# Two-layer gated decoder, one core: layer 1's down projection as three rounded products, with the weights' low parts streamed

## What is computed

```python
x = x + tanh(g_xattn[0]) * L0_xattn(layernorm(x), ctx, ctx)
# L0_ffn: of each sequence the k = 256 tokens with the highest score
scores = einsum('bld,d->bl', x, w_r) + b_r
_, idx = top_k(scores, k)
x_sel = take_along_axis(x, idx)
h = gelu(einsum('bkd,df->bkf', x_sel, w1) + b1)      # 512 -> 2048
out_sel = einsum('bkf,fd->bkd', h, w2) + b2          # 2048 -> 512: the down projection
out = zeros_like(x).at[batch, idx].set(out_sel)
x = x + tanh(g_ffn[0]) * L0_ffn(layernorm(x))
# then layer 2
```

## Time and profile before

| | us |
|---|---|
| median of 3 runs | 1008.98 |
| lowest, highest | 1005.02, 1009.32 |
| the profiled execution: its time | 1008.89 |
| the profiled execution: its span | 1007.1 |

### The profile page before, as it was taken

The page is one execution under the profiler, slowest core; times in us unless marked ns, Lnnn a source line. Parts: engine busy times, 40 slices in busy tenths (PEclk is TensorE's granted clock), DMA queues, the critical chain, the costliest instruction groups (busy, mean ns, idle before and its releaser), DMA issues.

```text
span 1007.1 us, 15849 instructions
## 1 busy us (share of the span) xinstructions
PE 899.4 (89%) x5592; PEld 586.9 (58%) x5592; DVE 678.4 (67%) x1893; ACT 574.5 (57%) x1098; POOL 82.2 (8%) x101
## 2 busy tenths in 40 slices
PE   3989998999999888799898999899999898999777
PEld 2868775667677463567444566544566544566433
DVE  4996771524241063699786799787699787699793
ACT  4545333455553032689546689547688547688543
POOL 2000213021120003200100000010000010000000
PEclk9999999999999989899999999999999999999979
DMA  6344566443350048710179210169210159300001
GB/s 192 130 159 139 196 230 230 147 141 111 106 206 24 21 152 179 151 43 1 43 153 182 84 43 2 44 131 194 94 43 2 43 117 202 100 1 2 1 1 42
DMA packets 52270, 102.82 MB, mean 102 GB/s; under 512 B 8924, under 2 KB 8924, under 8 KB 50656
## 3 DMA queue, kind: packets, MB, share of 16 engines
q1 hardware_dynamic: 39872, 71.88, 27.3%
q10 hardware_dynamic: 8160, 17.31, 5.2%
q0 software_dynamic: 4160, 12.62, 4.0%
HBM read 55.62 MB, written 14.75 MB: 70 GB/s over the span
## 4 chain that ended last, share of the span: by engine, by line
PE 36%; DVE 9%; issue 6%; ACT 5%; SPq 4%; DMA 3%; POOL 1%; DVEq 0%; ACTq 0%; POOLq 0%
PE psum L1517 7%; PE psum L1485 6%; PE psum L1590 6%; PE psum L1534 5%; PE psum L1560 5%; SPq L1186 4%; ACT probs L1333 3%; DMA k<-k_lo 3%; PE psum L1452 1%; PE psum L1576 1%; PE psum L1543 1%; DVE xn L1911 1%; DVE stats L1906 1%; DVE stats L57 1%; POOL q L1170 1%
## 5 line engine op out<-in xcount | busy, mean ns | idle before, releaser
L1333 ACT ACTIVATE probs<-psum,neg_max 128x512 f32<-128x512 f32 x256 | 174.7, 691 | 46.1 <-DVE neg_max L1801 46.1
L1801 DVE CUSTOM_DVE_ANT_0 psum<-psum,m_in 128x512 f32<-128x512 f32 x256 | 174.0, 704 | 17.2 <-issue 17.2
L1517 PE MATMUL psum<-ident,probs 128*128 128x128 f32 x1024 | 153.3, 274 | 0.0
L1485 PE MATMUL psum<-k,q 128*128 128x512 f32 x256 | 125.1, 494 | 15.5 <-ACT probs L1333 7.5
L1517 PEld LDWEIGHTS psum<-ident,probs 128*128 128x128 f32 x1024 | 127.1, 140 | 19.5 <-issue 1.8
L674 PE MATMUL psum<-w_sb,hT 128*128 128x512 f32 x256 | 117.5, 604 | 5.5 <-ACT hT L566 5.5
L1831 DVE COPY probsT<-psum 128x512 f32<-128x512 f32 x128 | 87.9, 687 | 4.0 <-PE psum L1517 2.8
L1324 ACT COPY probsT<-psum 128x512 f32<-128x512 f32 x128 | 75.1, 587 | 20.4 <-PE psum L1517 20.4
L594 PE MATMUL psum<-xselT_hi,w_hi 128*128 128x256 f32 x256 | 81.8, 320 | 1.6 <-ACT xselT_hi L501 1.6
L1485 PEld LDWEIGHTS psum<-k,q 128*128 128x128 f32 x256 | 48.8, 191 | 52.3 <-ACT probs L1333 32.8
L674 PEld LDWEIGHTS psum<-w_sb,hT 128*128 128x128 f32 x256 | 46.9, 192 | 55.3 <-issue 48.2
(11 more groups left out here) (237 smaller groups left out, 1536.8 us busy)
## 6 DMA issues: line engine op xcount, KB each, us to landing
bw_raw<-in_L_ffn_W_dram ACTq DMA_DIRECT2D x16, 1024.0 KB, 5.3
c_in<-in_ctx_dram SPq DMA_DIRECT2D x8, 1024.0 KB, 5.3
k<-k_hi SPq DMA_DIRECT2D x24, 256.0 KB, 5.9
k<-k_lo SPq DMA_DIRECT2D x24, 256.0 KB, 6.9
q<-q_hi SPq DMA_DIRECT2D x48, 128.0 KB, 3.9
q<-q_lo SPq DMA_DIRECT2D x48, 128.0 KB, 3.5
xres<-in_x_dram SPq DMA_DIRECT2D x4, 1024.0 KB, 5.9
w_raw<-in_L_ffn_w_dram POOLq DMA_DIRECT2D x4, 1024.0 KB, 5.6
```

The source lines that it names most:

```text
L1333: act.activation(probs[:, u % 4, :], psum[u % SCORE_BANKS][:, :], ACT.Exp, scale=-1.0, bias=neg_max[:, u:u + 1], accum_out=prob_sum[:, nt, ...
L1485: pe.matmul(psum[u % SCORE_BANKS][:, :], q4[:, h, nt * P:(nt + 1) * P], k4[:, h, :], start=True, stop=True).then_inc(score_psum, 1)
L1517: mm = pe.transpose(turn_bank(u)[:, l * P:(l + 1) * P], probs[:, u % 4, l * P:(l + 1) * P], ident[:, :])
L1801: dve.tensor_tensor_reduce(bank[:, :], bank[:, :], m_in[:, nt, :], -1.0, LOWEST, ALU.add, ALU.min, neg_max[:, u:u + 1]).then_inc(masked_re ...
```

## The change

1. **Down projection.** `down` becomes `three` on 128x512 tiles: 12 float32r matmuls for a pair where there were 4 float32 ones. ACT makes `h_hi` (`hidden_high`, a 128x512 copy behind each pair's gelu), DVE `h_lo` (`hidden_low`); both lie in a ring of 3.
2. **Weights of it.** `w2_hi` stays in SBUF (ACT, `w2_high`, 8 copies of 128x1024, 3 of them before the first up). The low parts don't fit: for each of the 32 pairs SP loads 512 KB of w2 again (`load_w2`, a ring of 3, each waiting for the down that used the slot, three pairs earlier), and DVE subtracts (`w2_low`, 128x1024).
3. **PE's order.** up(g) for g = 0 to 31 without a break between batches, and down(g - 2) behind it. DVE's additions to `x_sel` (`put_together`) stand behind `hidden_low` of the next batch's pair 1.
4. **DVE's list** is dealt out by pairs (`route_next`, `round_next`): hidden_low, put_together, a piece of the routing, w2_low.
5. **Order of batches** 0, 3, 1, 2 (`ORDER`), since only `xres[0]` stays free of the rings; batches 1 and 2 are loaded again (`load_x1`).
6. **First routing** spread a pair later: PE's `spread_scores` at pair 3, ACT's at pair 4; in later batches pair 2 and 3.
7. **load_selected** moves from SP to POOL.
8. **Hand-over.** The last two scatters move from POOL's list in layer 1 to the head of POOL's list in layer 2. wk is loaded once down(30) has ended (`w2_used`), wv once the last down has; layer 1 no longer waits for either, PE waits before their transposes.

```diff
+                def load_w2(g):
+                    k, p = divmod(g, PAIRS)
+                    if g >= RING:
+                        k0, p0 = divmod(g - RING, PAIRS)
+                        if p0 == PAIRS - 1:
+                            sp.wait_ge(osel_psum, (k0 + 1) * JT)
+                        else:
+                            sp.wait_ge(w2_used, k0 * (PAIRS - 1) + p0 + 1)
+                    i = g % RING
+                    sp.dma_start(w2_raw[:, 2 * i:2 * i + 2, :], w2[2 * P * p:2 * P * (p + 1), :].rearrange("(f p) c -> p f c", p=P)
+                                 ).then_inc(w2_loaded[i], 16)
...
+                sp.wait_ge(w2_used, (B - 1) * (PAIRS - 1) + PAIRS - 2)
+                load_weight(2, wk, sh.wk_loaded)
+                sp.wait_ge(osel_psum, B * JT)
+                load_weight(1, wv, sh.wv_loaded)
...
+                for g in range(RING):
+                    w2_high(g)
                 selected_highs(0)
...
+                for g in range(B * PAIRS):
+                    k, p = divmod(g, PAIRS)
+                    if k + 1 < B and p == (3 if k else 4):
+                        spread_scores(k + 1, psum[4])
+                    gelu(g)
+                    hidden_high(g)
+                    if RING <= g < PAIRS:
+                        w2_high(g)
+                    if k + 1 < B and p == PAIRS - 1:
+                        selected_highs(k + 1)
+                    weights(g)
...
+                def up(g):
+                    k, p = divmod(g, PAIRS)
...
+                    if g >= 2:
+                        pe.wait_ge(h_ready, 2 * (g - 1))
...
+                def down(g):
+                    k, p = divmod(g, PAIRS)
+                    pe.wait_ge(h_lo_ready, g + 1)
+                    pe.wait_ge(w2_lo_ready, g + 1)
+                    if p == 0 and k:
+                        pe.wait_ge(x2_ready, k * JT)
+                    for i in range(2):
+                        f = 2 * p + i
                         for j in range(JT):
-                            mm = pe.matmul(psum[j][:, :], hT[:, f % RING, j * P:(j + 1) * P], w2_sb[:, f, :],
-                                           start=(f == 0), stop=(f == FT - 1))
+                            mm = three(psum[j][:, :], [h[g % RING][:, i, j * P:(j + 1) * P] for h in (h_hi, h_lo)],
+                                       [w2_hi[:, f, :], w2_lo[:, 2 * (g % RING) + i, :]], f == 0, f == FT - 1)
...
+                for g in range(B * PAIRS):
+                    k, p = divmod(g, PAIRS)
+                    up(g)
+                    if k + 1 < B and p == PAIRS - 1:
+                        if k == 1:
+                            pe.wait_ge(bw_inv_ready, 2)
+                        turn_selected(k + 1)
+                    weights(g)
+                    if g >= 2:
+                        down(g - 2)
+                    if k + 1 < B and p == (2 if k else 3):
+                        spread_scores(k + 1, psum[4])
+                down(B * PAIRS - 2)
+                down(B * PAIRS - 1)
...
+                for g in range(B * PAIRS):
+                    k, p = divmod(g, PAIRS)
+                    hidden_low(g)
+                    if k and p == 1:
+                        put_together(k - 1)
+                    if g == 1:
+                        w2_low(2)
+                    if k + 1 < B:
+                        route_next(k, p, link)
...
+                    if g >= RING:
+                        w2_low(g)
+                put_together(B - 1)
...
+                for j in range(sh.ids.shape[2]):
+                    pool.indirect_dma_start(
+                        sh.x_mid[sh.last_batch][:, :], bass.IndirectOffsetOnAxis(ap=sh.ids[:, B - 1, j:j + 1], axis=0),
+                        sh.x_sel_last[:, j, :], None).then_inc(sh.x2_stored[sh.last_batch], 16)
...
-                for i, (w, ready) in enumerate(((wk_in, linear_act_ready), (wv_in, linear_dve_ready))):
+                for i, (w, loaded, ready) in enumerate(((wk_in, sh.wk_loaded, linear_act_ready),
+                                                        (wv_in, sh.wv_loaded, linear_dve_ready))):
+                    pe.wait_ge(loaded, 16)
```

More of the change, by code:

```diff
@@ L168, in layer0 @@
         XW = C + 8
+        RING = 3
+        ORDER = [0] + [B - 1] + list(range(1, B - 1))
         xres = sb("xres", [P, 3, T, C])
@@ L225, in layer0 @@
         xn_sel = at("xn_sel", [P, JT, XW], F32, parts_at + 8 * K)
-        RING = 8
-        hT = at("hT", [P, RING, KEEP], F32, sig_at)
+        h_at = (sig_at, sig_at + 4 * K, sh.front + 20 * K)
+        h_hi = [at(f"h_hi{i}", [P, 2, KEEP], F32R, h_at[i]) for i in range(RING)]
+        h_raw = [at(f"h_raw{i}", [P, 2, KEEP], F32, h_at[i] + 2 * K) for i in range(RING)]
+        h_lo = [at(f"h_lo{i}", [P, 2, KEEP], F32R, h_at[i] + 2 * K) for i in range(RING)]
         score = sb("score", [P, T])
@@ L254, in layer0 @@
         w1_lo_ready = sem("w1_lo_ready")
-        w2_loaded = [sem(f"w2_loaded_{i}") for i in range(4)]
+        w2_loaded = [sem(f"w2_loaded_{i}") for i in range(RING)]
+        w2_hi_ready = sem("w2_hi_ready")
+        w2_lo_ready = sem("w2_lo_ready")
+        w2_used = sem("w2_used")
+        h_hi_ready = sem("h_hi_ready")
+        h_lo_ready = sem("h_lo_ready")
+        x1_loaded = sem("x1_loaded")
         x_loaded = sem("x_loaded")
@@ L379, in _ @@
                 select(0)
+                load_selected(0)
                 fetch(0)
@@ L664, in up @@
                     mm.then_inc(h_psum, 1)
-                def down(b, pair):
-                    pe.wait_ge(h_ready, b * FT + 2 * pair + 2)
-                    if pair == 0 and b:
-                        pe.wait_ge(x2_ready, b * JT)
-                    if b == 0 and pair % 2 == 0:
-                        pe.wait_ge(w2_loaded[pair // 2], 16)
-                    for f in (2 * pair, 2 * pair + 1):
+                def down(g):
[5 more added lines that the diff above has]
+                    for i in range(2):
+                        f = 2 * p + i
@@ L837, in cross_attend @@
                         w1_lows(range(4))
+                        for g in range(2):
+                            w2_low(g)
                     if b == 1:
@@ new lines, in round_weights, with whole_weights @@
+                def round_weights(i, link):
+                    w = (wq_w, wo_w)[i]
+                    for t in range(CT_):
+                        dve.tensor_scalar(w[:, t, :], w[:, t, :], sh.w_inv[:, i, t:t + 1], ROUND,
+                                          ALU.mult, ALU.add).then_inc(link.sem, 1)
+                        link.count += 1
+                def whole_weights(i, link):
+                    link.wait()
+                    if i == 0:
+                        dve.wait_ge(x_sel_ready, B)
+                        dve.wait_ge(x2_stored[ORDER[B - 2]], 16 * JT)
+                    link(dve.tensor_scalar(w_whole[:, i, :, :], (wq_w, wo_w)[i][:, :, :], -ROUND, None, ALU.add))
@@ new lines, in w2_low, with hidden_low @@
+                def w2_low(g):
+                    i = g % RING
+                    dve.wait_ge(w2_loaded[i], 16 * (g // RING) + 16)
+                    dve.wait_ge(w2_hi_ready, min(g + 1, PAIRS))
+                    f = 2 * (g % PAIRS)
+                    dve.tensor_tensor(w2_lo[:, 2 * i:2 * i + 2, :], w2_raw[:, 2 * i:2 * i + 2, :],
+                                      w2_hi[:, f:f + 2, :].bitcast(F32), ALU.subtract).then_inc(w2_lo_ready, 1)
+                def hidden_low(g):
+                    dve.wait_ge(h_hi_ready, g + 1)
+                    dve.tensor_tensor(h_lo[g % RING][:, :, :], h_raw[g % RING][:, :, :],
+                                      h_hi[g % RING][:, :, :].bitcast(F32), ALU.subtract).then_inc(h_lo_ready, 1)
@@ L879, in bw_unit, with put_together @@
                     dve.reciprocal(bw_inv[:, i:i + 1], sh.bw_mean[:, i:i + 1]).then_inc(bw_inv_ready, 1)
[L881 to L889 removed]
+                def put_together(k):
+                    dve.wait_ge(x_sel_ready, k + 1)
+                    for j in range(JT):
+                        dve.wait_ge(osel_psum, k * JT + j + 1)
+                        dve.scalar_tensor_tensor(x_sel[k % 2][:, j, :], psum[j][:, :], gate_f0, x_sel[k % 2][:, j, :],
+                                                 ALU.mult, ALU.add).then_inc(x2_ready, 1)
@@ new lines, in route_next @@
+                def route_next(k, p, link):
+                    n = k + 1
+                    if p == 0:
+                        if n == 1:
+                            route_stats(link, n)
+                        route_norm(link, n)
+                    elif p == 1:
+                        scores(link, n)
+                        if k == 1:
+                            bw_unit(0)
+                    elif p == 2 and k == 0:
+                        w1_lows(range(6, PAIRS))
+                    elif p == 3:
+                        ranks(link, n, range(2))
+                    elif p == 4:
+                        ranks(link, n, range(2, T))
```

253 lines of the change are left out of this document (119 added, 134 removed).

## The result

The changed kernel takes 998.73 us (median of 5 runs, 997.36 to 999.49) where the kernel before takes 1006.09 beside it (5 runs, 1004.70 to 1009.32): a ratio of 0.9915, 95% interval 0.9895 to 0.9935. Set again beside the kernel before in a later comparison it took 997.84 for 1008.16, a ratio of 0.9904 (0.9873 to 0.9934). The forecast was 998, a fall of 11.1; measured is a fall of 7.4 in the first comparison and of 10.3 in the second. The total was right; most of its terms were not, and that they cancelled is luck.

A forecast was written before the change was run, and what follows sets the result against it. It took ACT's chunk chain to set the pace up to M (192.7 us) and PE only behind it. Stage -5.8 and hand-over -5.3 made -11.1 on 1008.89: about 998 us, range 991 to 1004, with the rivals 984 to 1009.

The forecast's parts named there:

- The down projection: 12 float32r matmuls take 2.73 us for 3.44 per pair; 22.7 us over all 32 if PE set the pace throughout.
- M': Time at which ACT ends the eighth chunk sum in the changed kernel: 195.6 us, against 192.7 before; bounds 184.4 and 202.8.
- rival 1: PE's pace rules at once: M' at 187, no clock lost, PE's end 329.7, time 986 us; chance 0.25.
- The idle spell at down(8): PE idle for nearly 8 us before batch 2's first down in order, waiting for put_together(0), with low clock behind it.
- 4.2 + 2.5 us: Costs at M': 4.2 us from M' through put_together's additions, 2.5 us lost to half clock after PE's idle time.
- The later first spread costs nothing: Spreading the first routing a pair later is free: ACT's slots are long there and the rows are needed at pair 7.
- The load by POOL: load_selected on POOL, with nothing queued in front but its own input, moves no landing by more than 0.5 us either way.
- DVE's extra work: In the stage DVE gets 61 us more, 138 of some 215; its in-order queue puts w2_low behind each piece of routing.
- down(g) comes two pairs behind up(g): That distance, 11 us, covers DVE's worst pair of some 6.6 us; without it, 1 to 2 us at a few pairs.
- The stage: Layer 1's feed-forward part: PE's last matmul at 341.8, some 5.8 us earlier than before.
- The hand-over: Between layers PE restarts 1.2 us behind DVE's end; context's transposes at +9.8 for +15.1, a gain of 5.3 us.
- With so short a pause the clock should stay at 1.00: At layer 2's start the clock stays at 1.00 instead of 0.50, sparing some 2 us of the transposes.

The follow-up runs named there:

- float32 run: Changed kernel with the down projection again one float32 matmul per tile, low parts made but not multiplied: 1013.71 us, ratio 1.0062 to the kernel before.
- the run with `w2_low` first: Changed kernel with w2_low moved ahead of the pair's piece of routing in DVE's list: 1001.08 us, ratio 0.9934 to the kernel before.
- early context: Changed kernel with the context of layer 2's first batch loaded in layer 1, behind the last up: 998.98 us, and 997.88 us when run again.
- scatters back: Changed kernel with the last two scatters back at the end of layer 1's list on POOL: 998.77 us, ratio 0.9898 to the kernel before.
- halves: Changed kernel with chunks of slots 1 to 8 loaded and summed as two halves, each reloaded once summed: 994.41 us, ratio 0.9863 to the kernel before.
- earlier copy: Changed kernel with ACT's copy of the first routing's scores at pair 3 again: 1000.00 us (three runs), ratio 0.9919 to the kernel before.

## Why the prediction was right, and where only by cancelling

- **The down projection: right.** 2.78 us for the 2.73 of the sum, 15.0 us for the stage by the float32 run. The prediction's 22.7 for PE's pace throughout, cut by a bound that holds PE up early, was the right shape.
- **M', the eighth sum: too late by 5.0 us (195.6, measured 190.6).** The first load's issue was right (129.6, 129.7). The term that was mis-sized is the load, 6.1 us for a measured 5.6 from issue to sum. The slot came out at 7.6 instead of 8.25, in spite of w2's stream beside it. M' lies about half way from the forecast to rival 1's 187.
- **The idle spell at down(8): wrong.** It didn't happen. At M' PE had 22 ups and 25 downs ahead, not 21 and 24, as it had already been held twice. put_together(0) ended at 195.1, and down(8) was due at 196.4. The 4.2 + 2.5 us in the sum were spent elsewhere, as 6.51 and 3.54 us of waits with low clock behind each, ahead of M'. One pair more (5.6) against 6.7 less of waiting and 1 less in the later slots make 2.1 less; behind M' it took 143.5 us for the forecast 146.2, so 0.6 stay unassigned.
- **"The later first spread costs nothing": wrong, and the step that hid the real bound.** I argued that the rows are needed at pair 7 only. They are then late by 3.54 us: the copy comes at 154.33 behind the chunk sum of slot 3, where at pair 3 it stands behind that of slot 2 and came at 145.6. The load by POOL was to move no landing by more than 0.5. That holds in later batches (a median of 4.2 us from issue for 3.8 in the earlier trace rows), not at this one, where it took 6.9 us while the DMA engines were busy for 0.8 of the time. I had costed the change of queue and not what is in the queues beside it; no run puts this load back on SP, so that it is the traffic and not the queue isn't shown.
- **DVE's extra work: right as a sum, wrong about the cover.** "down(g) comes two pairs behind up(g)" covers h_lo and w2_low as long as DVE's list doesn't stand still. It did for 5.95 us, and then the distance was too short. That wait cost nothing by itself, as the rows were later still (the run with `w2_low` first).
- **The stage: -5.8 forecast, -13.6 measured**, nearer to rival 1 (-17.9) than to the forecast. From 176.8 on PE set the pace, not from M' on.
- **The hand-over: the restart was right (1.1 us, forecast 1.2), POOL's drain too, SP's was short (0.12 us) as taken.** wv's transposes began at +5.5, in the bounds, and the context's at +10.5, forecast +9.8. What failed is that the gain of 5.3 was booked there. I followed the path to the context and no further: its own load was the last to land, the clock fell to 0.50 behind that wait, the keys took 15.66 us instead of 13.97, and the first score came only 1.1 us sooner (means of two). "With so short a pause the clock should stay at 1.00" held for that pause (1.00 until 345.1); the pause that counted was the next one. That the wait is the cause is shown by the early context, without it and at 1.00. But that run's 5 us were stopped at the next gate, the low parts of the queries. And the bounds of the sum don't fit each other: +8 to +11.5 for +15.1 is a gain of 3.6 to 7.1, not of 3 to 6.5.

The Trainium skill ("TensorE: Matmul & The Clock Gate", section What's actually happening) has low clock as the state that only activity releases; behind each wait of 2.6 us or more above, these traces agree. The Trainium skill's drains of some 12 ns ("VectorE: DVE Perf Modes", section The DRAIN you can't avoid) are those of a program's pre- and postamble. The drains at this barrier don't fit that figure on any engine that had just worked: 123 ns on SP, 807 ns on DVE, 5.9 us on POOL and 7.7 us with the scatters back.

- **Layer 2: not in the sum at all, +3.9.** It was taken to start earlier and run as before. First part and rest are 1.7 and 2.2 us longer.

So -13.6 and -1.1 and +3.9 and +0.7 stand where -5.8 and -5.3 were forecast.

**What stays open.** Why the rest of layer 2 falls on one or the other length; some 1 us between the rest in the kernel before (465.0, 465.8) and in the variants with the same lost clock (466.5 to 466.8), whose lists there are alike; and what the first part would be if the low parts of the queries were loaded sooner.

## What to carry to other kernels

When an engine gets faster, list every gate that it can now reach, with its time, and take the latest: here the gathered rows, the chunk sum and a low part lay within a few us of each other, and moving one brought 0 or 3 us according to the others. Moving an operation "one step later, since it isn't needed yet" is costed by what it then stands behind in its list. And a gain at a hand-over counts at the first point where the next stage is steady, not where the wait was: here a load 16 us behind the first score took it back. Cut both profiles at the same few events, and take a second profile of the kernel before, before a difference of 0.5% in an untouched stage is called chance.

## What the runs showed of the chip

- An engine's drain at the barrier isn't a constant: 0.12 us on SP, which had issued a load 0.4 us earlier that landed some 5 us later; 0.81 on DVE; and on POOL behind two scatters 5.0, 5.9 (in the changed kernel, at 294, where nobody waits) and 7.7 us. In all 13 profiles POOL's drain ends 1.5 to 1.7 us behind the landing of the second scatter, so its length is that of the scatters: it was 7.7 us where they landed beside the loads of wk and wv.
- Of a gain of 5 us at the hand-over between nothing and 4 us are left 190 us later. Hand-over and first part together are 190.9 to 194.8 us with the early context (four profiles), 194.2 and 195.5 in the changed kernel, while the hand-over alone ranges from 53.5 to 63.2.
- A wait of 2.31 us for the context had the clock at 0.50 behind it in one profile (halves, from 342.7) and at 1.00 in another (float32 down, from 358.6). One and the same wait can cost clock or not.
- Two-input operations from SBUF on DVE and on POOL took turns, and the later one paid. `w2_low`, 1.22 us otherwise, took 3.41 where POOL had started 0.05 us before it, and ended 1.1 us behind POOL's end; where it started first it took 1.21, and POOL's 3.47 for 2.38. `h_lo`, 0.69 otherwise, took 2.39 in the run with the earlier copy. DVE's one-input `stats_r<-xres` kept its 0.68 us beside the same operation on POOL (kernel before, 131 to 133.5). From the changed kernel:

```profile
182.58 2.38 POOL L391 TENSOR_TENSOR x_sel<-x_sel,b_row 128x1024 f32<-128x1024 f32 x1 [2.82 <-DMA x_sel<-x_mid_dram,ids]
182.63 3.41 DVE L938 TENSOR_TENSOR w_lo<-w_raw,w_hi 128x1024 fp32r<-128x1024 f32 x1
...
232.09 1.21 DVE L938 TENSOR_TENSOR w_lo<-w_raw,w_hi 128x1024 fp32r<-128x1024 f32 x1
232.10 3.47 POOL L391 TENSOR_TENSOR x_sel<-x_sel,b_row 128x1024 f32<-128x1024 f32 x1 [4.96 <-DMA x_sel<-x_mid_dram,ids]
```
